# Gates of layer 0's experts on their inner units instead of on their outputs, in a four-layer kernel on one core

## The reference

```python
x = x + _L0_xattn_ref(_layernorm(x), ctx_768, ...)
x = x + _L0_ffn_ref(_layernorm(x), ...)

def _L0_ffn_ref(hidden_states, router_w, actor_w1, actor_b1, actor_w2, actor_b2, gate_w, up_w, down_w):
    probs = softmax(hidden_states @ router_w.T)            # 8 experts
    a_h = gelu(hidden_states @ actor_w1.T + actor_b1)      # 50 units
    actor_logits = clip(a_h @ actor_w2.T + actor_b2, -30, 30)
    sampled_k = argmax(actor_logits) + 1                   # 1 to 6
    scores = where(rank(probs) < sampled_k, probs, 0)
    for e in range(8):                                     # every expert on every token, I = 336
        g = hidden_states @ gate_w[e].T
        u = hidden_states @ up_w[e].T
        y = (silu(g) * u) @ down_w[e].T
        out = out + scores[..., e:e + 1] * y
```

## Time and profile before

| | us |
|---|---|
| median of 3 runs | 2266.57 |
| lowest and highest run | 2265.08, 2271.86 |
| profiled execution | 2266.21 |
| its span | 2263.6 |
| PE busy | 1895.3 (84%) |
| DVE busy | 1248.3 (55%) |
| ACT busy | 1052.3 (46%) |
| POOL busy | 886.3 (39%) |

### The profile page before, as it was taken

How to read it: one execution, slowest core, us unless ns; L and a number is a source line. 1 busy time by engine, 2 the same in 40 slices (tenths; PEclk the granted TensorE clock), 3 DMA queues, 4 the chain that set the end, 5 groups by cost and what they waited for, 6 DMA issues and landing times.

```text
span 2263.6 us, 36101 instructions
## 1 busy us (share of the span) xinstructions
PE 1895.3 (84%) x11048; PEld 1355.9 (60%) x11048; DVE 1248.3 (55%) x3395; ACT 1052.3 (46%) x3404; POOL 886.3 (39%) x891
## 2 busy tenths in 40 slices
PE   3999989989999886888887899887899888877664
PEld 1555555555555675666565778665788544654553
DVE  2457466575664423455566667666667545564423
ACT  1444444434344222666655444566444555765211
POOL 1565776756756404103332130332120333225315
PEclk9999999999999998998898899998999756995666
DMA  4504205114010487544000747100756102641566
GB/s 139 199 4 162 73 13 171 62 42 110 17 60 28 140 238 224 153 132 123 29 23 14 259 163 253 33 23 17 271 178 225 30 23 65 178 128 37 144 173 178
DMA packets 158555, 256.44 MB, mean 113 GB/s; under 512 B 22636, under 2 KB 94510, under 8 KB 157998
## 3 DMA queue, kind: packets, MB, share of 16 engines
q1 hardware_dynamic: 146078, 228.96, 32.5%
q0 software_dynamic: 12288, 25.19, 3.7%
HBM read 190.11 MB, written 77.08 MB: 118 GB/s over the span
## 4 chain that ended last, share of the span: by engine, by line
PE 53%; DVE 15%; ACT 9%; issue 8%; POOL 6%; SPq 4%; DMA 3%; POOLq 0%; DVEq 0%; ACTq 0%
PE up L875 9%; PE Y L954 7%; PE up L936 6%; PE A L760 6%; PE Y L884 5%; ACT prob L1118 4%; PE B L768 4%; PE D L778 3%; PE up L941 3%; DVE nmax L1304 2%; POOL list L1728 2%; ACT probT L1124 2%; DVE xn L1273 1%; DMA wg<-list 1%; POOL hid L1783 1%
## 5 line engine op out<-in xcount | busy, mean ns | idle before, releaser
L1783 POOL TENSOR_TENSOR hid<-tg,uc 112x512 f32<-112x512 f32 x192 | 248.7, 1296 | 185.6 <-ACT uc L1173 147.3
L1728 POOL DMA_INDIRECT list<-xn,pos x192 | 190.6, 993 | 315.5 <-DVE pos L1446 264.1
L1124 ACT ACTIVATE probT<-B 128x512 f32<-128x512 f32 x256 | 156.4, 611 | 328.8 <-PE B L768 328.8
L884 PEld LDWEIGHTS Y<-wd,hid 112*128 112x128 f32 x1536 | 201.6, 194 | 143.5 <-issue 111.0
L1520 DVE SCALAR_TENSOR_TENSOR tg<-tg,up 112x512 f32<-112x512 f32 x192 | 131.4, 684 | 226.3 <-ACT tg L1169 225.8
L884 PE MATMUL Y<-wd,hid 112*128 112x128 f32 x1536 | 208.7, 279 | 33.5 <-DVE ytmp L1530 19.5
L1169 ACT ACTIVATE tg<-up 112x512 f32<-112x512 f32 x192 | 114.8, 598 | 261.6 <-PE up L875 217.2
L768 PEld LDWEIGHTS B<-const,prob 128*128 128x128 f32 x1024 | 134.7, 163 | 151.7 <-issue 149.2
L1304 DVE TENSOR_REDUCE nmax<-A 128x4 f32<-128x512 f32 x128 | 88.1, 688 | 239.4 <-PE up L760 239.4
L768 PE MATMUL B<-const,prob 128*128 128x128 f32 x1024 | 195.3, 323 | 17.9 <-ACT probT L1124 17.9
L875 PE MATMUL up<-x2T,wg 128*112 128x512 f32 x384 | 204.9, 615 | 2.1 <-DVE tg L1520 2.1
(11 more groups left out here) (236 smaller groups left out, 4123.4 us busy)
## 6 DMA issues: line engine op xcount, KB each, us to landing
w_tile<-wt SPq DMA_DIRECT2D x45, 768.0 KB, 4.5
list<-w_tile SPq DMA_DIRECT2D x21, 1536.0 KB, 13.4
w_tile<-wt SPq DMA_DIRECT2D x45, 512.0 KB, 3.9
w_tile<-wt SPq DMA_DIRECT2D x50, 321.0 KB, 3.1
wg<-list SPq DMA_DIRECT2D x248, 64.0 KB, 3.2
list<-wu SPq DMA_DIRECT2D x248, 64.0 KB, 3.3
wd<-wt SPq DMA_DIRECT2D x17, 768.0 KB, 4.8
wd<-wt SPq DMA_DIRECT2D x17, 512.0 KB, 3.9
```

Of the source, the lines that this page charges most:

```text
L884: mm = pe.matmul(Y4[:, t, :], hid[0:rows, i % HRING, t * P:(t + 1) * P], wd[0:rows, i, :], start=(c == 0 and t == 0), stop=(c == PER_UNIT[ ...
L1124: act.activation(probT[:, (2 * r + i) % 4, :, :], B4[:, :, :], ACT.Copy).then_inc(probT_done.sem, 1)
L1728: pool.indirect_dma_start(out=list_to(K, g)[:, :], in_=xn2[:, t, :], in_offset=None, out_offset=bass.IndirectOffsetOnAxis(ap=pos[:, g, s, ...
L1783: pool.tensor_tensor(hid[0:rows, i % HRING, :], tg[0:rows, i % 2, :], uc[0:rows, i % 2, :], ALU.mult).then_inc(hid_ready.sem, 1)
```

## The change

The gate of an expert is now multiplied into its hidden rows, before the down product, so that all 24 chunks can be summed in one bank. The gates must for that lie along the tokens in the columns, repeated on 112 rows.

- `turn_gates`, at step 21: PE turns `gates` (four transposes) into bank A, and ACT copies it to `gT` (8 rows x 512).
- `spread_gates`, two experts at each of the steps 22 to 25: PE multiplies `gT` by `one_row`, a table of 8 x 112 that has ones in row e, so that gate e stands on 112 rows of bank A or B; ACT copies that to `wide_gates`. Steps 24 and 25 fall into steps 0 and 1 of the next trip (`late`). A spread product waits until the copy two before it is done.
- ACT no longer copies the up half. DVE multiplies it by `wide_gates` instead, straight from the bank, into `uc`.
- `down_product`: the down weights are the stationary operand and the hidden rows move, one product of 512 columns for a chunk, all 24 summed in Y, features in the rows.
- After the last chunk (steps 1 and 2 of the next trip) ACT copies Y, PE turns it back with four transposes into bank D (`turn_sum`), and DVE adds it to x once (`add_sum`). `weigh_expert` and `add_expert` are gone.
- Layer 0's parts from the cosines on move up by one or two steps, layer 1's by up to two.
- DVE makes `one_row` once, with one copy before the first statistics.

```diff
@@ steps, both shared
         def due(trip, s):
             n = TRIP * trip + s - LAG
-            last = TRIP * GROUPS
-            down = n if 0 <= n < last else None
-            e = n // PER_UNIT[0] - 1
-            return down, e if n % PER_UNIT[0] == 0 and 0 <= e < last // PER_UNIT[0] and n <= last else None
+            return n if 0 <= n < TRIP * GROUPS else None
+
+        def late(trip, s):
+            return (trip, TRIP + s) if 0 <= trip < GROUPS and s < LAG else (None, None)
@@ tensor
             def down_product(g, i):
...
+                if i == 0:
+                    pe.wait_ge(y_read.sem, y_read.at(0, g, 0))
+                mm = pe.matmul(Y[:, :], wd[0:rows, i, :], hid[0:rows, i % HRING, :],
+                               start=(i == 0), stop=(i == CHUNKS[0] - 1))
...
-                    mm = pe.matmul(Y4[:, t, :], hid[0:rows, i % HRING, t * P:(t + 1) * P], wd[0:rows, i, :],
-                                   start=(c == 0 and t == 0), stop=(c == PER_UNIT[0] - 1), skip_group_check=True)
...
+            def turn_sum(g):
+                pe.wait_ge(y_read.sem, y_read.at(0, g, 1))
+                if g:
+                    pe.wait_ge(rstep.sem, rstep.at(1, g - 1, 2))
+                for t in range(T):
+                    mm = pe.transpose(D4[:, t, :], yT[:, t * P:(t + 1) * P], ident)
+                mm.then_inc(y_ready.sem, 1)
+
+            def turn_gates(g):
+                pe.wait_ge(gates_done[0].sem, gates_done[0].at(0, g, 1))
+                pe.wait_ge(act1.sem, act1.at(0, g, 1))
+                for t in range(T):
+                    mm = pe.transpose(A[0:EXPERTS, t * P:(t + 1) * P], gates[:, g % 2, t, :], ident)
+                mm.then_inc(wide_psum.sem, 1)
+
+            def spread_gates(g, e):
+                if e < 2:
+                    pe.wait_ge(wide_done.sem, wide_done.at(0, g, 1))
+                else:
+                    pe.wait_ge(wide_done.sem, wide_done.at(0, g, e))
+                pe.matmul((A, B)[e % 2][0:ROWS[0], :], one_row[:, e, :], gT, start=True, stop=True)\
+                    .then_inc(wide_psum.sem, 1)
...
+                    group, sl = late(g, s)
+                    if group is not None:
+                        layer0(group, sl)
+                    if g > 0 and s == LAG:
+                        turn_sum(g - 1)
@@ scalar, layer0 and hidden
+                if s == 21:
+                    act.wait_ge(wide_psum.sem, wide_psum.at(0, g, 1))
+                    act.activation(gT, A[0:EXPERTS, :], ACT.Copy).then_inc(wide_done.sem, 1)
+                if s >= 22:
+                    for e in (2 * (s - 22), 2 * (s - 22) + 1):
+                        act.wait_ge(wide_psum.sem, wide_psum.at(0, g, e + 2))
+                        act.activation(wide_gates[:, e, :], (A, B)[e % 2][0:ROWS[0], :], ACT.Copy)\
+                            .then_inc(wide_done.sem, 1)
+
+            def evacuate_sum(g):
+                act.wait_ge(y_ready.sem, y_ready.at(0, g, 1))
+                act.activation(yT, Y[:, :], ACT.Copy).then_inc(y_read.sem, 1)
...
-                act.activation(uc[0:rows, i % 2, :], up[b][0:rows, :], ACT.Copy).then_inc(up_read[b].sem, 1)
@@ vector
+            dve.tensor_copy(one_row, ident[0:EXPERTS, 0:EXPERTS].unsqueeze(2).to_broadcast([EXPERTS, EXPERTS, ROWS[0]]))
...
+                dve.wait_ge(u_ready.sem, u_ready.at(0, g, i + 1))
+                dve.wait_ge(wide_done.sem, wide_done.at(0, g, i // PER_UNIT[0] + 2))
+                dve.tensor_tensor(uc[0:rows, i % 2, :], up[b][0:rows, :], wide_gates[:, i // PER_UNIT[0], :], ALU.mult)\
+                    .then_inc(up_read[b].sem, 1)
+
+            def add_sum(g):
+                dve.wait_ge(y_ready.sem, y_ready.at(0, g, 2))
+                dve.tensor_tensor(x[:, g, :, :], x[:, g, :, :], D4[:, :, :], ALU.add).then_inc(x_added.sem, 1)
```

More of the change, by code:

```diff
@@ L216, in build @@
         own = front[:, 3 * N:5 * N]
+        wide_gates = front[0:ROWS[0], 5 * N:13 * N].rearrange("p (e n) -> p e n", e=EXPERTS)
+        gT = front[0:EXPERTS, 13 * N:14 * N]
         def gating(name, at, shape):
@@ L386, in build @@
         hid_ready = signal("hid_ready", [CHUNKS[0]], 2)
-        y_ready = signal("y_ready", [EXPERTS])
-        y_read = signal("y_read", [EXPERTS], 1)
-        x_added = signal("x_added", [EXPERTS], 1)
+        y_ready = signal("y_ready", [2])
+        y_read = signal("y_read", [1], 1)
+        x_added = signal("x_added", [1])
+        wide_psum = signal("wide_psum", [1 + EXPERTS])
+        wide_done = signal("wide_done", [1 + EXPERTS])
         mask_done = signal("mask_done", [0, 1, 1, 1])
@@ L892, in trip @@
                         up_product(g, s)
-                    down, _ = due(g, s)
+                    down = due(g, s)
                     if down is not None:
                         down_product(*divmod(down, TRIP))
+                    group, sl = late(g, s)
[3 more added lines that the diff above has]
+                        turn_sum(g - 1)
                     tile_turns(turns)
@@ L1136, in layer0 @@
                     read_context0(g)
-                if s == 14:
+                if s == 12:
                     evacuate_norm(0, g, LN2)
-                if s == 15:
+                if s == 13:
                     act.wait_ge(act1_psum.sem, act1_psum.at(0, g, 1))
                     act.activation(ay, A[0:ACTOR, :], ACT.Identity, bias=ab1[:, 0:1]).then_inc(act1.sem, 1)
-                if s == 17:
+                if s == 15:
                     exp_logits(0, g)
-                if s == 18:
+                if s == 16:
                     act.wait_ge(act_pool.sem, act_pool.at(0, g, 2))
                     act.activation(ath, ay2, ACT.Tanh, scale=GELU_A).then_inc(act1.sem, 1)
+                if s == 21:
+                    act.wait_ge(wide_psum.sem, wide_psum.at(0, g, 1))
+                    act.activation(gT, A[0:EXPERTS, :], ACT.Copy).then_inc(wide_done.sem, 1)
+                if s >= 22:
+                    for e in (2 * (s - 22), 2 * (s - 22) + 1):
+                        act.wait_ge(wide_psum.sem, wide_psum.at(0, g, e + 2))
[4 more added lines that the diff above has]
+                act.activation(yT, Y[:, :], ACT.Copy).then_inc(y_read.sem, 1)
             def layer1(g, s):
+                if s == 6:
+                    evacuate_norm(1, g, LN1)
                 if s == 7:
-                    evacuate_norm(1, g, LN1)
+                    read_queries1(g)
                 if s == 8:
-                    read_queries1(g)
+                    read_keys1(g)
                 if s == 9:
-                    read_keys1(g)
-                if s == 10:
                     read_values1(g)
-                if s == 12:
+                if s == 11:
                     exponentials1(g)
@@ L1178, in trip @@
                         hidden(g, s)
+                    group, sl = late(g, s)
+                    if group is not None:
+                        layer0(group, sl)
+                    if g > 0 and s == LAG - 1:
+                        evacuate_sum(g - 1)
                     if group0 is not None:
@@ L1537, in trip @@
                 for s, chunk, group0, group1, s1, turns in in_trip(g):
-                    _, expert = due(g, s)
-                    if expert is not None:
-                        weigh_expert(*divmod(expert, EXPERTS))
                     if chunk is not None:
                         hidden(g, s)
+                    if g > 0 and s == LAG:
+                        add_sum(g - 1)
                     tile_turns(turns)
@@ L1545, in trip @@
                         layer0(group0, s)
+                    if g > 0 and s == OVER - 1:
+                        layer1(g - 1, s)
                     if group1 is not None:
@@ L1784, in hidden @@
                                    ALU.mult).then_inc(hid_ready.sem, 1)
-            def add_expert(g, e):
-                pool.wait_ge(y_read.sem, y_read.at(0, g, e + 1))
-                pool.wait_ge(x_added.sem, x_added.at(0, g, e))
-                pool.sem_inc(alone, 1)
-                pool.tensor_tensor(x[:, g, :, :], x[:, g, :, :], ytmp[:, e % 2, :, :], ALU.add)\
-                    .then_inc(x_added.sem, 1)
             def trip(g):
                 for s, chunk, group0, group1, s1, _ in in_trip(g):
-                    _, expert = due(g, s)
-                    if expert is not None:
-                        add_expert(*divmod(expert, EXPERTS))
                     if chunk is not None:
```

91 lines of the change are left out of this document (42 added, 49 removed).

## The result

The changed kernel takes 2325.11 us (2323.71 to 2327.86) against 2267.59 us (2265.08 to 2271.86) for the kernel before: a ratio of 1.0254, 95% interval 1.0231 to 1.0277. It is slower by 58 us; forecast were 2307 us, 41 more, within 2276 to 2342. The profiled execution took 2323.71 us, its span is 2321.9.

The account below looks back on a forecast made before the run. PE was taken as the bound, with idle pieces. Lead-in 9.6, trip 0 5, six full trips 24, trip 7 0 and clock 2 sum to +40.6 on 2266.2: 2307 us, range 2276 to 2342.

Parts of the forecast that it names:

- Spread product, 0.86: On PE, each of a group's eight spread products takes 0.86 us, priced as an up product.
- rival c: Spread products of 8 rows cost only 0.53 us and the idle time is gone: 2255 us; chance 0.08.
- Down product, 0.89 to 0.86: On PE, each of 192 chunks' down products falls from 0.89 to 0.86 us, 0.72 us less in a trip.
- Lead-in, 12.5 later and 2.9 refunded: Before the first chunk: gates and table of ones delay the start, PE's fast pace returns 2.9: +9.6 us (7 to 12).
- Trips 1 to 6, +4.0 each: Six full trips: 7.04 us more PE work less 3.0 of idle time each, +24 us in all.
- Clock, +2 (0 to 8): Denser PE work brings more stretches with a lower granted clock: 2 us added (0 to 8).
- DVE carries it: DVE takes 24 more products a trip, +11.8 us, about 68 of 89 us busy; it fits on the whole.
- Rival (b): DVE becomes the bound and its delays add 8 us in each full trip: +78, 2344 us; chance 0.14.
- rival a: Idle time pays for the added work, six full trips cost 0.1 us each: +10, 2276 us; chance 0.12.
- Rival (d): No change to speak of: idle time pays and spread products cost, say, 0.75 us: 2269 us; chance 0.06.
- Trip 7 and the rest, 0: Last trip: +3.2 us of work fills PE's waits for POOL's scatters, 0 (-2 to +3); everything after 763 us unchanged.

Follow-up runs that it names:

- block of four: Changed kernel with a group's spread products issued four in step 23, four in step 25: 2339.74 us (8 rows), 2296.85 us (128 rows).
- full-row version: Changed kernel with the spread products on all 128 rows of the array, rows 8 to 127 zero: 2291.45 us, ratio 1.0112.
- kernel without spreading: Changed kernel without turning and spreading the gates or ACT's copies for it; wide_gates constant, gates not applied: 2261.47 us, ratio 0.9983.

## Why the prediction was right, and where it was not

The sign, the range and the driver were right: PE was the bound, got more work than it had idle time, and the surplus is the loss. The 2325 us lie 18 above the forecast 2307, from one term that was mis-sized (the clock) and one price that was missing (the change of rows); more idle time paid than I thought, which hides part of both. By stretches: lead-in and trip 0 +7.4 against the sum, trips 1 to 6 +5.0 (31.0 against 24 and 2 for the clock), trip 7 +2.1, the rest +3.2.

**Spread product, 0.86.** Right for a product (0.86 inside a block of four), but not for its place. I gave it the price of an up product between up products and did not ask what a change of shape costs. The piece above shows 0.18 us at each change: two changes for each of 30 pairs, 10.8 us, 1.44 in a full trip. The full-row version, where a spread product has no such change beside it, saves 11.8 us of work and other together. In trips 1 to 6 work grew by 49.9 us; forecast were 6 x 7.04 = 42.2, and 6 x 1.44 = 8.6 is the difference but for 1 us. The Trainium skill ("TensorE: Matmul & The Clock Gate", Step-by-step: what each phase is for) says that PE pulls a weight load ahead of running products if the row groups don't conflict or if it goes to the background buffer. The trace agrees between products of 112 and 128 rows (load 0.42 us ahead) and shows no such overlap between 8 or 64 rows and these.

**Spread product at 0.53 (rival c).** Fell: it takes 0.86 where it is cheapest. The two 32-row products that run side by side have no bearing on products that share their rows.

**Down product, 0.89 to 0.86.** Right.

**Lead-in, 12.5 later and 2.9 refunded.** The first half came out at 10.2 (the gates were ready a little earlier than I had them, 58.87 against 60.2). The second half is the step that failed: "since PE then runs fast by the time it reaches the up products". It did not run fast until 87.44, and instead of 2.9 us given back trip 0 has 7.0 us more of slow (9.96 against 2.92). The runs show what is in the way, the 8 rows: with 128 rows the doubled rows end at 67.10 and trip 0 has no slow time. The lead-in and trip 0 together should have given +14.6 and gave +22.0; full rows give +11.3 (10.5 and 0.8), less than the sum said.

**Trips 1 to 6, +4.0 each.** They came 93.5 to 99.4 us apart, not 92 to 94, and grew by 31.0 us: work 49.9, slow 10.2, idle -31.1, other 2.0. The idle time left is 2.6 us a trip (15.8 over six) against the 4 that I found. The 1.3 at the actor's logits came out (8.7 us in seven waits); the up product behind the gating waits 0.7 instead of 1.3; the 1.5 before the next group's first normalization show up once, with 0.7. Work up and idle down nearly cancel: in the full-row version the six trips grew by 8.6 us.

**Clock, +2 (0 to 8).** Mis-sized, the largest error: slow grew by 17.2 us in all. The 7.0 of trip 0 are shown to come from the 8 rows, and blocks of four show that these rows can bring PE to the slow pace in the middle of a trip, while it is busy. Of the 10.2 us in trips 1 to 6 of the changed kernel some 7 are the four stretches right behind the first pair of spread products, where no kernel without 8- or 64-row spreads has one. So the rows explain these as well, as far as one profiled execution of each kernel can tell; for the rest the cause stays open. The total alone would not tell: it is 23.9 us here, 13.7 before, and 10.0 and 18.5 with 128 and 112 rows, but some 22 where DVE gates the tokens, a kernel with no 8-row product (mean granted clock over trips 1 to 6: 0.95 here, 0.98 before, 0.94 there), and each is one profiled execution.

**DVE carries it.** On the whole, yes: DVE's busy time is 63 us in trip 3 (forecast 68), and PE waits for it about 14 us in all. L1481's successor L1536 takes 1.49 us in the median (418/1488/1496 ns) against 2.7, as said. The new product L1581 takes 673 to 693 ns in all 192 cases, so POOL does not slow it, as forecast. But "That fits on the whole" looks at DVE's busy time, and the sum holds DVE's lag behind PE only in the 4 us of idle time a trip. Where PE has no spread products, the move costs 31 us. Rival (b) was right in its mechanism and wrong in its place: in the changed kernel the added PE work stands where PE would wait for DVE.

**Idle pays for the work (rival a).** It did, further than I gave it a chance: 35.4 us of it went, against 61.1 of work. In the full-row version, without the price of the row changes and with 10.1 us of slow, the outcome is +25 us, between rival (a)'s +10 and the forecast's +41. Rival (d) needed products below 0.86 and fell with (c).

**Trip 7 and the rest, 0.** Trip 7 grew by 2.1 us up to its last down product: work 4.0, idle -1.7. Within the given -2 to +3. The 3.2 behind it are open, as said.

Reading the split again, the change cannot win through PE: it removes 5.8 us of down products (192 x 0.03) and adds 64 products of 0.86. What it would bring if the gates came free is seen in the kernel without spreading: nothing, unless DVE's extra product goes too.

## To carry to other kernels

Before you add small products to a PE that is the bound, count the changes between row heights (0.18 us each here) as well as the products, and try filling unused rows with zeros where that is free: it made this change 34 us cheaper, with the same products, columns and copies. Work added to the bound hides the lag of the engine behind it, so test a moved step both with and without that cover. Idle time in front of the bound pays for added work only until the next wait is late; here 35 of 61 us were paid.

## What the runs showed of the hardware

- A product of 8 rows and 512 columns in fp32 takes 0.86 us, as one of 128; a change between 8 or 64 rows and 112 or 128 costs 0.18 us (starts 0.95 us apart instead of 0.86, twice), and between 112 and 128 nothing.
- Products with 8 rows keep PE at its slow pace or bring it there while PE is busy throughout. In the lead-in the doubled rows end at 87.44 us with 8 rows in pairs, 74.80 with 64, 68.65 with 112 and 67.10 with 128; where the blocks of four leave four up products without a spread between them, they end at 71.03 with 8 rows too. In blocks of four the granted clock falls at 13 of 15 blocks with 8 rows, to 0.53 behind the second product of the one shown, and at none of 15 with 128. The 64-row products of layer 0's cosines are another place of falls with no idle time ahead. Why few rows do this, no run here shows.
